# A transformer layer kernel: four pairs of tiles normalised ahead of its steps in place of eight, running states added straight from PSUM, and six one-hot columns a step in place of eight

## The reference, cut to what matters

```python
xn = layernorm(x)
q, k, v = xn @ Wq, xn @ Wk, xn @ Wv              # 16 heads of 16
local = softmax(mask(q_l k_l^T / 4)) v_l          # 4 heads, windows of 128 and the one before
q_g, k_g = softmax(q_g), elu(k_g) + 1             # 12 heads, blocks of 64 tokens
ctx = cumsum(k_g^T v_g per block) / (cumsum(sum k_g) + 1e-6)   # shifted by one block
glob = q_g @ ctx
attn = concat(local, glob) @ Wo + bo
scores = xn @ router_w.T                          # 8 experts, the top 2 of each token
ffn = sum of the two experts' gelu(xn @ w1.T) @ w2.T, weighted
out = x + attn + ffn
```

## Time and profile before

| | us |
|---|---|
| median of 3 runs | 804.63 (802.73 to 806.93) |
| the profiled execution, its own time | 808.07 |
| its span, first to last instruction | 806.3 |
| PE busy | 688.7 (85%) |
| DVE busy | 464.5 (58%) |
| ACT busy | 403.9 (50%) |
| POOL busy | 411.5 (51%) |
| mean granted TensorE clock | 0.928 of full |

### The profile page before, as it was taken

One profiled execution on the slowest core, in us unless ns is written; L12 is line 12 of the kernel. 1 busy time (PEld: TensorE's weight loads), 2 busy tenths in 40 slices (PEclk: granted clock), 3 DMA queues, 4 the chain that ended last, 5 costly groups with the idle time before them and its releaser, 6 DMA issues.

```text
span 806.3 us, 21562 instructions
## 1 busy us (share of the span) xinstructions
PE 688.7 (85%) x6874; PEld 542.5 (67%) x6875; DVE 464.5 (58%) x1600; ACT 403.9 (50%) x1128; POOL 411.5 (51%) x429
## 2 busy tenths in 40 slices
PE   1689999999558686887589999999999999999883
PEld 1456666666335454554378888888888888888763
DVE  5789899887788878787532344344433333333331
ACT  4568888888335454555243344444334433343331
POOL 5647777767434344347224555555554555444522
PEclk9989999999767777788799999999999999999998
DMA  8034343343111312122124444444444444443421
GB/s 267 8 132 133 119 143 109 107 128 104 65 48 47 74 53 66 54 80 52 43 51 69 74 78 77 79 77 77 74 77 74 75 74 75 74 71 58 63 43 20
DMA packets 87991, 64.26 MB, mean 80 GB/s; under 512 B 54675, under 2 KB 81556, under 8 KB 87924
## 3 DMA queue, kind: packets, MB, share of 16 engines
q1 hardware_dynamic: 73204, 43.69, 20.0%
q0 software_dynamic: 13632, 18.91, 15.4%
q10 hardware_dynamic: 1088, 0.79, 0.3%
HBM read 36.08 MB, written 17.96 MB: 67 GB/s over the span
## 4 chain that ended last, share of the span: by engine, by line
PE 49%; issue 21%; POOL 18%; DVE 6%; SPq 2%; DMA 2%; ACT 1%; POOLq 0%; DVEq 0%
PE bank L283 25%; PE bank L1198 21%; POOL stage L837 3%; SPq L689 2%; POOL xb L830 2%; POOL ke L817 2%; POOL w2l L839 2%; POOL cum L828 2%; POOL w1l L839 2%; POOL atl L824 1%; POOL rows L744 1%; POOL rstd L799 1%; DMA stage<-xin 1%; DVE stats L1225 1%; DVE w1h L1238 1%
## 5 line engine op out<-in xcount | busy, mean ns | idle before, releaser
L283 PE MATMUL bank<-stage,w1h 128*128 128x256 f16 (+1 forms) x1248 | 198.1, 266 | 6.5 <-DMA stage<-xin 5.1
L283 PE MATMUL bank<-stage,w1l 128*128 128x256 f16 (+1 forms) x624 | 164.0, 265 | 0.0
L1198 PE MATMUL bank<-w2h,pt 128*128 x568 | 154.9, 273 | 5.9 <-issue 4.8
L1198 PE MATMUL bank<-w2h,spare 128*128 x568 | 154.8, 273 | 0.0
L1198 PE MATMUL bank<-w2l,pt 128*128 x568 | 154.8, 273 | 0.0
L283 PEld LDWEIGHTS bank<-stage,w1h 128*128 x1248 | 114.5, 98 | 26.9 <-issue 9.3
L1020 ACT ACTIVATE pt<-ss 128x512 f16<-128x512 f32 (+1 forms) x78 | 41.8, 583 | 149.1 <-PE bank L1198 149.1
L872 POOL DMA_INDIRECT out<-attn,rows_to x35 | 59.0, 1685 | 74.9 <-DMA out<-attn,rows_to 48.7
L872 POOL DMA_INDIRECT out<-res,rows_to x36 | 57.6, 1600 | 70.1 <-DMA stage<-rows 50.7
L824 POOL TENSOR_TENSOR atl<-attn,ath 128x128 f16<-128x128 f32 x32 | 13.7, 427 | 150.1 <-ACT ath L956 150.1
L1013 ACT ACTIVATE ss<-bank 128x512 f32<-128x512 f32 (+1 forms) x78 | 42.2, 548 | 69.7 <-remote 59.3
(11 more groups left out here) (249 smaller groups left out, 1673.1 us busy)
## 6 DMA issues: line engine op xcount, KB each, us to landing
stage<-w1c SPq DMA_DIRECT2D x16, 512.0 KB, 3.7
stage<-w2c SPq DMA_DIRECT2D x16, 512.0 KB, 3.8
xb<-x SPq DMA_DIRECT2D x32, 128.0 KB, 3.6
out<-res SPq DMA_DIRECT2D x32, 128.0 KB, 3.5
stage<-xin SPq DMA_TRANSPOSE x144
stage<-rows SPq DMA_TRANSPOSE x140
w1h<-x SPq DMA_DIRECT2D x8, 256.0 KB, 4.3
xin<-x SPq DMA_DIRECT2D x16, 128.0 KB, 3.8
```

The costliest lines, as they stand in the source:

```text
L283: ins = pe.matmul(dst, lhs(a, k), rhs(c, k), start=(n == 0), stop=(n == len(terms) - 1))
L1198: ins = pe.matmul(bY[h][:, 0:D], (hh, hl)[a][:, f, h * P:(h + 1) * P], (w2h, w2l)[c][:, DS(which * (FC * D) + f * D, D)], start=(f == a == ...
```

## The change

- The prologue takes four pairs of tiles. The other twelve pairs are taken in steps 0 to 11, a pair in each (begun in step t, the low halves in t+1, turned in t+2, router scores in t+3). x is loaded in pairs into eight slots, and each tile's rows are stored by a DMA of their own. POOL makes its constants ahead of the first pair.
- The weights of the projections are split at the third pair in place of the fourth.
- PE keeps the states of the two blocks in one bank, its two parts in different places of the step. DVE adds each to the running sum straight from PSUM (`state0` at the start of its step, `state1` after `atl`), unmasked. POOL masks both with one instruction of 128x388, between L837 and L839 of its step, in place of `cum`. PE's `lin` waits for it (`mask_in`).
- The softmax of q is no longer divided on DVE (L1391). DVE divides the global attention instead, when it copies it out: `lrow` moves from ACT to the very start of DVE's step.
- `rrec` moves to the end of DVE's previous step, ahead of the one-hots.
- ACT takes DVE's half of the copy of transposed probabilities from step 14 on.
- The routing comes four steps earlier (14, 15, 16). The one-hots are made 6 columns a step, in steps 17 to 27, still last in DVE's step. The gathers come in step 29.

```diff
-CH = 8
+CH = 6
...
-LEAD = 16
-AHEAD, WEIGHTS_AT = LEAD // 2, 3
+AHEAD, WEIGHTS_AT = 4, 2
+SLOTS = 8
...
-        def route_onehots(dve, i):
+        def route_onehots(dve, i, first, many):
...
-            for c in range(CH):
+            for c in range(first, min(first + many, columns_in(i))):
...
-            ins.then_inc(hot_in, 1)
+                dve.tensor_scalar(hot_blk[i % 2][:, c, :], sm["biota"], sm["blk"][:, k, tile:tile + 1],
+                                  sm["tok"][:, tile:tile + 1], ALU.is_equal, ALU.mult).then_inc(hot_in, 1)
 
...
-                    if t.t < LEAD // 4:
-                        store_ahead(t.t)
...
+                    if t.t < AHEAD:
+                        store_rows(t.t)
+                    if t.early(2):
+                        store_rows(t.early(2)[0] // 2)
+                    if SLOTS + t.t < PAIRS:
+                        sp.wait_ge(s["rl_in"], 2 * t.t + 2)
+                        load_x(SLOTS + t.t)
...
+                constants()
                 for q in range(AHEAD):
-                    rstd_of(2 * q, 2)
...
-                        rstd_of(t.t + LEAD, 1)
+                    if t.early(0):
+                        rstd_of(t.early(0)[0] // 2)
...
-                        t.wait(s["new_in"], -2)
-                        t.wait(s["att_ps"], -2)
-                        pool.tensor_tensor(cum[b][:], cum0[b][:], new1[b][:], ALU.add).then_inc(s["cum_in"], 1)
...
-                        lower_half(t.t + LEAD - 1)
+                    for u in t.early(1):
+                        lower_half(u)
...
+                    if t.has(-1):
+                        b = t.row(-1)
+                        t.wait(s["state1_in"], -1)
+                        t.wait(s["lin_ps"], -3)
+                        pool.tensor_tensor(state[b][:], raw[b][:], ctx_mask[:].unsqueeze(1).to_broadcast([P, 2, CTX]),
+                                           ALU.mult).then_inc(s["mask_in"], 1)
+                    if t.has(0):
                         t.wait(s["stage_up"], 0)
                         pool.tensor_tensor(lo[:, DS(t.window(0) * F, F)], stage[m][:], hi[:, DS(t.window(0) * F, F)],
                                            ALU.subtract).then_inc(s["stage_lo"], 1)
...
-                    if t.has(-2):
...
-                        act.activation(lrow[:], b_att[:, 0:D], ACT.Copy).then_inc(s["lrow_in"], 1)
-                    if t.early(LEAD - 2):
-                        copy_turned(t.t + LEAD - 2, b_xnt)
+                    if t.early(2):
+                        copy_turned(t.early(2)[0], b_xnt)
...
+                        if half_ == 0 and t.early(2):
+                            copy_turned(t.early(2)[1], b_xnt)
...
+                        if t.t >= ACT_TURNS:
+                            act.activation(pt[:, 0:2, :, :], b_s[0][:].rearrange("p (h c n) -> p h c n", h=2, c=2),
+                                           ACT.Copy).then_inc(s["pta_in"], 1)
...
+                        t.wait(s["mask_in"], -2)
...
-                    if t.early(LEAD - 3):
-                        router_of(t.t + LEAD - 3)
+                    for u in t.early(3):
+                        router_of(u)
...
+                    if t.early(2):
+                        pe.wait_ge(s["rl_in"], t.early(2)[0] + 1)
+                        turn_x(t.early(2)[0], b_xnt)
...
+                    if t.early(2):
+                        pe.wait_ge(s["rl_in"], t.early(2)[1] + 1)
+                        pe.wait_ge(s["xt_in"], t.early(2)[0] + 1)
+                        turn_x(t.early(2)[1], b_xnt)
...
+                    if t.has(-1) and t.has(1):
+                        t.wait(s["state1_in"], -1)
+                        add_to_state(t, 1)
...
+                for q in range(AHEAD):
+                    begin(q)
...
+                    if t.has(-2):
+                        b = t.row(-2)
+                        t.wait(s["lin_ps"], -2)
+                        t.wait(s["att_ps"], -3)
+                        dve.tensor_tensor(heads(lrow[:]), heads(b_att[:, 0:D]), spread(qrec[b][:], DH), ALU.mult)\
+                           .then_inc(s["lrow_in"], 1)
+                    if t.has(0):
+                        b = t.row(0)
+                        if t.t < 2:
+                            dve.wait_ge(raw_zero, 2)
+                            dve.memset(raw[b][:, 0, 0:CTX:CTX - 1], 1e-6).then_inc(s["state0_in"], 1)
+                        else:
+                            t.wait(s["ctx1_ps"], -2)
+                            t.wait(s["mask_in"], -2)
+                            dve.tensor_tensor(raw[b][:, 0, :], b_state[:, b * CTX:(b + 1) * CTX], raw[b][:, 1, :], ALU.add)\
+                               .then_inc(s["state0_in"], 1)
...
-                    if t.has(-2):
-                        b = t.row(-2)
-                        t.wait(s["prob1"], -2)
-                        dve.reciprocal(rrec[b][:], rsum[b][:]).then_inc(s["rrec_in"], 1)
-                    if t.early(LEAD):
-                        u = t.t + LEAD
-                        dve.wait_ge(x_loaded[u % 2], 16 * ((u - LEAD) // 2 + 1))
-                        mean_of(xin[u % 2][:, 0:D], u)
-                        variance_of(u)
-                        guarded(u, 1)
+                    if t.early(0):
+                        begin(t.early(0)[0] // 2)
...
-                        t.wait(s["ctx_ps"], -1)
-                        t.wait(s["cum_in"], -3)
-                        dve.tensor_tensor(new0[b][:], b_ctx[:, D:D + CTX], ctx_mask[:], ALU.mult).then_inc(s["new0_in"], 1)
-                        dve.tensor_tensor(new1[b][:], b_tok1[:, D:D + CTX], ctx_mask[:], ALU.mult).then_inc(s["new_in"], 1)
-                        dve.reciprocal(rden[b][:, :, 0], cum[b][:, 0:CTX:CTX - 1])
-                        t.wait(s["new0_in"], -1)
-                        dve.tensor_tensor(cum0[b][:], cum[b][:], new0[b][:], ALU.add).then_inc(s["cum0_in"], 1)
-                    if t.has(-1):
-                        b = t.row(-1)
-                        t.wait(s["cum0_in"], -1)
-                        dve.reciprocal(rden[b][:, :, 1], cum0[b][:, 0:CTX:CTX - 1]).then_inc(s["rden_in"], 1)
-                    if t.early(LEAD):
-                        t.wait(s["rl_in"], LEAD - 2)
-                        scaled(xin[t.row(LEAD)][:, 0:D], t.t + LEAD)
+                        t.wait(s["ctx0_ps"], -1)
+                        dve.tensor_tensor(raw[b][:, 1, :], b_state[:, b * CTX:(b + 1) * CTX], raw[b][:, 0, :], ALU.add)\
+                           .then_inc(s["state1_in"], 1)
+                        t.wait(s["state1_in"], -1)
+                        dve.reciprocal(rden[b][:].rearrange("p g u -> p u g"), raw[b][:, :, 0:CTX:CTX - 1])\
+                           .then_inc(s["rden_in"], 1)
+                    for u in t.early(0):
+                        scaled(u)
...
-                    if t.has(-1):
+                    if t.has(-1) and t.t < ACT_TURNS:
...
-                        dve.reciprocal(qrec[b][:], qsum[b][:]).then_inc(s["qrec_in"], 1)
-                        t.wait(s["qrec_in"], 0)
-                        dve.tensor_tensor(heads(qs[b][:, 0:GD]), heads(qs[b][:, 0:GD]), spread(qrec[b][:], DH),
-                                          ALU.mult).then_inc(s["qn_in"], 1)
+                        dve.reciprocal(qrec[b][:, 0:12], qsum[b][:])
+                        dve.reciprocal(qrec[b][:, 12:16], qsum[b][:, 8:12]).then_inc(s["qrec_in"], 1)
+                    if t.has(-1):
+                        b = t.row(-1)
+                        t.wait(s["prob1"], -1)
+                        t.wait(s["att_ps"], -3)
+                        dve.reciprocal(rrec[b][:], rsum[b][:]).then_inc(s["rrec_in"], 1)
+                    if HOT <= t.t < HOT + BATCHES:
+                        route_onehots(dve, t.t - HOT, 0, CH)
...
-                    if HOT <= t.t < HOT + BATCHES:
-                        route_onehots(dve, t.t - HOT)
```

More of the change, by code:

```diff
@@ L111, in block_kernel @@
         negmax, rsum, rrec = pair("negmax", [P, LH]), pair("rsum", [P, LH]), pair("rrec", [P, LH])
-        cum, cum0 = pair("cum", [P, CTX]), pair("cum0", [P, CTX])
-        new0, new1 = pair("new0", [P, CTX]), pair("new1", [P, CTX])
+        state = pair("state", [P, 2, CTX])
+        raw = pair("raw", [P, 2, CTX])
         rden = pair("rden", [P, 2, 2])
@@ L234, in has, with early @@
                 return 0 <= self.t + off < NT
-            def early(self, off):
-                return LEAD <= self.t + off < NT
+            def early(self, lag):
+                q = AHEAD + self.t - lag
+                return (2 * q, 2 * q + 1) if AHEAD <= q < PAIRS else ()
             def row(self, off):
@@ L338, in block_kernel, with all_rows_stored @@
         gathered = [sem(f"gathered{m}") for m in range(2)]
+        def all_rows_stored(eng):
+            for n in range(SLOTS):
+                eng.wait_ge(rows_stored[n], 32 * (PAIRS // SLOTS))
         def route_reset(pool):
```

(41 more changed lines are left out.)

170 lines of the change are left out of this document (71 added, 99 removed).

## The result

The changed kernel takes 867.0 us (median of 4 executions, 866.4 to 868.85) against 804.2 us (802.73 to 806.93) for the kernel before in the same session: the ratio is 1.078, 95% interval 1.0747 to 1.0814. The profiled execution has a span of 865.0 us, 58.7 more than before (the medians are 62.8 apart, since the profiled execution of before was one of its longest), and a mean granted clock of 0.899 where it was 0.928.

The account below looks back on a forecast made before the run. It took PE's wait for POOL's late mask, and for `lrow` behind the one-hots, as the bound, experts unchanged: -10 + 4 + 49 + 2.6 + 24.5 = +70 on 808.1, 878, predicted as an 875 us median; range 817 to 898.

Parts of the forecast that it names:

- prologue: Before the steps: four pairs at 2.16 us each and router scores of eight tiles leave it; -10 us (bounds -8 and -12).
- steps 0 to 2: First three steps: the same mask wait once in two steps, and two tiles of work; +4 us (0 to 9).
- steps 3 to 12: Ten early steps: PE waits for POOL's mask, then a lowered clock; 13.7 us each, +49 (bounds +37 and +60).
- step 13: The step after the early ones: the mask wait without low halves, 11.3 us for 8.7; +2.6.
- steps behind it: After step 13, up to the experts: routing, one-hot and plain steps, 264.4 us against 239.9; +24.5 (bounds -2 and +32).
- experts: Last stretch, from 398.7 us on in the kernel before, not touched by the diff: counted as unchanged.
- a granted clock near 0.7 in 50 to 190 us: Sign expected in the early part of the changed kernel, with early steps of 12.5 to 14.8 us.
- The rival in which the clock stays up: PE's idle time leaves the clock high: early steps 12.5 us, one-hot steps 13.2, +45, 850 us; chance 0.16.
- The one-hot steps: Eleven steps: L1391's stall handed on to a one-hot, PE waits for `lrow` behind them; 14.2 us each, 156 together.
- The rival in which the one-hots hold POOL off: DVE's one-hots get the shared port first: one-hot steps of 11.8 us, 849 us in all; chance 0.13.
- work decides: Each step costs its busiest engine's work: early steps 9.2 us, eleven one-hot steps 113, -31, 774 us; chance 0.09.
- the last ones: Six plain steps behind the one-hot steps, with the mask wait ahead of the gathers: 62 us.

Follow-up runs that it names:

- experiment 4: Changed kernel with 50 matmuls nobody reads put ahead of PE's wait for the mask in steps 2 to 13: 853.8 us, ratio to before 1.061.
- experiment 1: Changed kernel with POOL's masking of the state moved ahead of its `locl`: 804.6 us, ratio to before 0.998.
- experiment 7: Changed kernel with POOL's mask first and one-hots ahead of DVE's masks, three pairs normalised ahead in place of four: 775.6 us, ratio to before 0.961.
- experiment 8: Changed kernel with POOL's mask first and one-hots ahead of DVE's masks, six pairs normalised ahead in place of four: 779.6 us, ratio to before 0.967.
- experiment 3: Changed kernel with both POOL's mask moved ahead of `locl` and DVE's one-hots moved ahead of its masks: 773.0 us, ratio to before 0.959.
- experiment 5: Changed kernel with POOL's subtraction L841 run on 64 of its 1024 columns in the one-hot steps: 838.1 us, ratio to before 1.042.
- experiment 2: Changed kernel with DVE's one-hots moved from the end of its step to ahead of its masks: 839.2 us, ratio to before 1.041.

## Why the prediction was right, term by term

The direction, the two causes and the size are as predicted: 867.0 against 875. That the sum is so near is helped by errors that cancel, named below. By its own terms, us of span:

| term | predicted | measured | from |
|---|---|---|---|
| prologue | -10 | -12.9 | first projections at 23.21 (36.10) |
| steps 0 to 2 | +4 | -1.9 | from there to `res` of step 3: 24.2 (26.1) |
| steps 3 to 12 | +49 | +48.6 | 136.4 (87.8) |
| step 13 | +2.6 | +3.3 | 11.9 (8.7) |
| steps behind it | +24.5 | +23.7 | 263.6 (239.9) |
| experts | 0 | -2.0 | 405.6 (407.6) |
| sum | +70 | +58.7 | 865.0 (806.3) |

**The early steps** are right link by link. The mask was put at m+8.1 and ends at m+8.0, its duration at 0.97 us and is 0.94, PE's idle time at 3.2 us and is 2.62 (PE's last matmul ends at m+5.55, not at m+4.9), the step at 13.7 and is 13.70. The part that was a choice, 13.7 between 12.5 at full clock and 14.8 at half, is borne out by experiment 4, where the same wait without idle time gives 12.33. The reason given for it holds (full clock at first, and again before the next m); that it fits so closely is luck, since it was the middle between two bounds. One sign was put wrong: a granted clock near 0.7 in 50 to 190 us, where 0.88 was measured, 3.4 us at 0.50 in a step of 13.7. The rival in which the clock stays up had the right price for that case and the wrong condition.

**The one-hot steps** were put at 14.2 us and are 13.6 on average, since one in three has full clock between `lrow` and the next m; the two prices there, 2.35 and 3.5 us, are 2.45 and 3.44. The stall was handed on as said. The one-hots were to begin at m+6.1, and one was to get in between mask and L841. In four of the eleven steps they begin at m+4.65 already, inside L832, and the first four instructions end one after another with POOL's L832, mask, L841 and `ke` (0.79, 0.98, 2.18 and 0.61 us, from 305.23). In three the second instruction is the long one (2.16 us), and in four the first (1.95 or 1.96). The rival in which the one-hots hold POOL off didn't occur: L841 takes 2.12 to 2.14 us in every one of these steps. The Trainium skill (SBUF — State Buffer, Who interferes with whom) has it that the one that issues first holds the shared port for its whole instruction; by that rule, the traces agree where the order can be read, with the long one-hot 0.22 us behind L841 (293.56 and 293.78) or 0.08 behind in experiment 1. In the other seven steps the two starts lie within 0.02 us (306.83 and 306.84), and who was first isn't shown.

**The prologue and the first steps** are the mis-sized term: -6 predicted, -14.8 measured. I priced a pair at DVE's spacing, 2.16 us, and allowed 1.3 for router scores; experiments 7 and 8 give 3.2 to 3.3 for all that hangs on a pair. The mask's wait with which I charged steps 0 to 2 is there, once, 2.61 us (without it, in experiment 3, they take 21.7 us for 24.2). What I left out is the clock of before, which falls in these steps, while it stays at 1.00 in those of the kernel after:

```profile
50.71 0.72 PE L1111 MATMUL bank<-pt,val 128*32 128x128 f32 x16 [1.06 <-ACT lrow L920]
...
52.00:58.00 6.00, 6.00 (x42) 3.76 (x42) 4.45 (x20) 3.16 (x13) 1.43 (x3) 0.50 0.09 27
```

These are rows of the kernel before. PE waits 1.14 us ahead of 47.91, 0.29 ahead of 49.26 and 1.06 ahead of 50.71, and the clock is 0.50 from 51.1 to 58.0. (In both kernels the very first projections go at half pace, 128x384 matmuls 0.32 us apart where it is 0.17 later, though the granted clock is given as 1.00; that is the same on both sides.) No run takes this away alone, so how much of the difference it makes isn't shown.

**The steps behind step 13** came out at +23.7 for +24.5 because errors cancel: one-hot steps 6.5 us less than put, the routing steps 1.3 more, the last ones 4.4 more. These last were put at 62 us and took 66.4. Most of the difference is the step of the gathers, 15.98 us here and 12.94 in experiment 3. A row of its timeline and a stretch behind it:

```profile
420.33 0.79 PE L1072 MATMUL bank<-val,ke 64*128 64x129 f32 x2 [3.20 <-POOL ke L815]
```

```profile
421.60:424.80 3.20, 3.20 (x19) 2.09 (x17) 1.38 (x5) 0.00 (x1) 3.20 (x3) 0.50 0.00 0
```

The wait for `ke` behind the gathers is 3.2 us in both kernels; what differs is how long the clock stays low. In experiment 3 it is 1.00 again from 9.6 us into the step on, here still 0.61 on average in the last 3.2 us. It isn't a cost of the change: experiment 4 has the same instructions from step 14 on and needs 12.90 us for this step, with 3.4 us at half clock where there are 10.2 here, and experiment 8, with both moves, needs 15.97. What decides between the two lengths isn't shown.

**The faster rival, "work decides",** was put at 774, on two conditions: the mask ready before `lin`, and one-hots that meet no POOL instruction. Experiment 3 makes the first true and takes the one-hots out of PE's chain, and has 773.0. That it meets 774 so closely is partly luck: its early steps take 9.62 us where 9.2 were put, and its prologue and first steps gain more than was put.

## What to carry to other kernels

Price a moved instruction by when its result is ready, in the order of the engine that makes it, before counting what it takes: the mask takes 0.94 us and its place cost 62. When a wait is taken out of a chain, look at what now stands in its place behind the same blocker; `lrow` took over the wait of `rrec`, and moving `rrec` alone in the kernel before gave 21 us. And where the granted clock falls behind it, charge an idle PE twice, once for the wait and once for the slower matmuls: here 2.7 and 1.4 us in an early step.

## What the runs showed of the hardware

- Matmuls whose result nobody reads made the kernel faster: 50 of 124 columns in a wait, 2.87 us of PE a step, took an early step from 13.70 to 12.33 us, the granted clock of the stretch rising from 0.88 to 1.00.
- Half clock came after shorter idle times than the 3.29 us of the earlier trace rows: after 2.62 us in each of the ten early steps, after waits of 1.14, 0.29 and 1.06 us within 4 in the kernel before, for 6.8 us, and once after waits of 1.65 us in four, for 10.2 us (experiment 7). In experiment 5 waits of 1.61 and 0.53 us in each step of 10.84 left it at 1.00, and in experiment 2 waits of 1.78 and 0.46 in each of 10.95. So the length of one idle time alone doesn't tell.
- A DVE instruction on one fp16 operand (a one-hot, 0.24 us) took up to 2.18 us when it met POOL's 2.12 us subtraction, and ended with it. In the steps read each one that meets a POOL instruction pays so, four in turn in the step from 300.58, and a shorter POOL instruction costs less (0.79 and 0.98 us behind those of 1.04 and 0.94).
